# Pads of the self-attention's stacks filled in the prologue, and the first rows of maxima sent ahead of the third and fourth stack

## The chip, the cores and the metric

The kernel runs on one core of a Trainium2 chip. The metric is the device time of one execution in microseconds (us). Each kernel is executed several times and the median counts.

## What is computed

Two layers on x (2 batches, 1024 tokens, 256 features) and a context of 77 tokens per batch, everything in float32. The first layer is a cross-attention to the context, 16 heads of 16 features, with a residual. The second is a decoder block: self-attention over the 1024 tokens, cross-attention to the context, and a feed-forward part of 1024 features.

```python
# layer 0
x = merge(softmax(Q K^T / 4) V) + x                 # Q from x, K and V from the context
# layer 1
qn = layernorm(x);  x = x + out_proj(self_attention(qn))
xn = layernorm(x);  x = x + out_proj(cross_attention(xn, context))
xn = layernorm(x);  x = x + gelu(xn @ w1.T + b1) @ w2.T + b2
```

## The kernel before

**Attentions and steps.** The program is one stream for each engine, written out by hand and tied together by semaphores. It has three attentions: A0 (layer 0), A1 (self-attention) and A2 (cross-attention of layer 1). An attention works on groups of four heads (QUAD); there are eight groups, 0 to 3 for the first batch and 4 to 7 for the second. Each group has two query blocks of 512 tokens, so there are 16 query blocks q, with q = 2g and 2g + 1 in group g. In A0 a step t is one query block: four score matmuls (line 813) into ST, four exponentials on ScalarE (line 947), the product with the values (line 829) into PV one step later, and the transposed result (line 778) one step after that. A0 has steps 0 to 15. A1 has eight steps for each query block, 128 in all.

**Stacks.** The scores are made with a stacked operand: six bands of 16 rows, which are parts of the queries split into bfloat16 pieces, and three more rows that hold the negated row maxima. TensorE thus subtracts the maximum within the score matmul. The bands of a group ("stack g") are read back from DRAM (`q_parts`) by six DMAs of 128 KB each (line 596). A0 has four stack buffers: stacks 0 and 1 lie in the tile V, stacks 2 and 3 in the tile `stacks`. The query parts are made in the prologue by `proj_q0` for four token blocks tb of 512 tokens, two chunks each. Each chunk is split on ScalarE, VectorE and (for tb = 3, by `ring_split_by`) GpSimd, and stored to `q_parts` by one DMA of 384 KB (line 563). GpSimd's two operations for a chunk are at lines 1308 and 1314.

**Maxima and rows.** A side task ("max", u) makes scores of 128 queries against the 77 keys for the four heads of a group (line 761, four matmuls) into SM, and VectorE reduces them (line 1063). Four such units (u = 4q to 4q + 3) give the maxima of query block q. GpSimd splits them into three parts (lines 1281 to 1287, written to `mp`), TensorE transposes these (line 772), VectorE copies them to `mrow` (line 1073), and SyncE (SP) sends them into the stack by a DMA of 12 KB (line 634). This is the side task ("rows", q), called "row q" below. The scores of step q wait for it. A step t of A0 has the units u = 12 + 4t to 15 + 4t and row t + 2. Units 0 to 11 and rows 0 and 1 come before step 0, in the order u0 to u5, row 0, u6 to u9, row 1, u10, u11. The first unit of a group waits for the six DMAs of its stack: u8 for stack 1, u16 (the first of step 1) for stack 2, u24 (step 3) for stack 3, u32 (step 5) for stack 4.

**Order of SP's queue.** All of these DMAs are issued by SP, one after the other. The order in front of A0 is the list BEFORE_A0; the other engines walk the same list and take only what is theirs, so moving a ("stack", ...) entry moves nothing but DMAs of SP:

```python
BEFORE_A0 = [("proj_k0", 0), ("proj_q0", 0), ("keys", "a0"), ("proj_q0", 1), ("stack", "a0", 0), ("vals_c", 0),
             ("values", "a0", 0), ("stack", "a0", 1), ("proj_q0", 2), ("stack", "a0", 2), ("proj_q0", 3),
             ("side", A0, 0, len(A0.before)), ("stack", "a0", 3)]
```

For SP, ("proj_q0", tb) means that it waits until each of the two chunks is split and then stores it. Within a step t SP sends row t + 2, then does the step's chores (in steps 0 to 3 a load of 512 KB of x into X, line 540), then the stack that has come due (stack 4 in step 2, stack 5 in step 4, stack 6 in step 6, stack 7 in step 8).

**Pads.** The rows of a stack between and behind the bands have to hold constants. `pad` (line 1185) fills 32 partitions by 2048 floats on GpSimd; `padded` counts `pad_ready` up. The pads that A0 needs are filled at the very start. Those of A1 for the key buffers Kst[0] and Kst[1] and the query buffer Qst[0], which A0 does not use, are filled in A0's steps 0, 1 and 2 by the chores ("pads", "a1", n), two fills each; part 3 fills nothing. GpSimd does a step's maxima first and then its chores. The rest of A1's pads come after A0.

Of the kernel before, what the change touches and what calls it, by code (L numbers as in the profile page):

```python
# [38 lines left out]
NB = TOK // BLK  # L39
TPB = BLK // P  # L40
QUAD = 4
# [6 lines left out]
SROWS = len(BANDS) * HD  # L48
# [31 lines left out]
def one_in_two(first, work):  # L80
# [5 lines left out]


UNDER_A0 = {
    **{n: [("load", n), ("pads", "a1", n)] for n in range(NB)},
    8: [("load", 4), ("load", 5)],  # L90
    9: [("x1", 0)],
    10: [("norm", 0, 0), ("x1", 1), ("load", 6), ("load", 7)],
# [44 lines left out]
class Attention:  # L137
# [61 lines left out]
    def chores(self, t):  # L199
# [3 lines left out]
A0 = Attention(0, 1, CTX, lead=12, rows_ahead=2, rows_at=0, buffers=4, banks=4, under=UNDER_A0,  # L203
               split_by=("pool", "dve"), lag=(0, 1))
A1 = Attention(1, SEQ // P, P, lead=26, rows_ahead=1, rows_at=4, buffers=3, banks=2, under=UNDER_A1,
               split_by=("pool", "pool"), lag=(1, 2))
# [9 lines left out]


BEFORE_A0 = [("proj_k0", 0), ("proj_q0", 0), ("keys", "a0"), ("proj_q0", 1), ("stack", "a0", 0), ("vals_c", 0),
             ("values", "a0", 0), ("stack", "a0", 1), ("proj_q0", 2), ("stack", "a0", 2), ("proj_q0", 3),
             ("side", A0, 0, len(A0.before)), ("stack", "a0", 3)]  # L220
BEFORE_A1 = [("stack", "a1", 0), ("vals_s", 0), ("x1", 2), ("vals_s", 1), ("x1", 3),
             ("norm", 0, 2), ("side", A1, 0, 2), ("t_ln1", 2),
             ("norm", 0, 3), ("side", A1, 2, 4), ("t_ln1", 3), ("pads", "a1", NB)]
SPREAD = [(stage, tb, i, 1) for stage, tb in (("proj_q1", 2), ("proj_k1", 2), ("proj_q1", 3), ("proj_k1", 3))
          for i in range(KC)]
BEFORE_A1 += [w for i, chunk in enumerate(SPREAD) for w in (("side", A1, 2 * i + 4, 2 * i + 6), chunk)]
# [21 lines left out]
def xattn_kernel(nc, xT_d, x_d, cT_d, ident_d, cols_d, rows_d, wq0, wk0, wv0, sa_w, so_w,  # L248
# [8 lines left out]
    with ctx:  # L257
# [3 lines left out]
        def sem(name):  # L261
            return ctx.enter_context(nc.semaphore(name))
# [16 lines left out]
        Kst = [stacks[:, n, 0] for n in range(A1.buffers)]  # L279
        Qst = [stacks[:, n, 1] for n in range(A1.buffers)]  # L280
# [108 lines left out]
        st_done = sem("st_done")  # L389
# [776 lines left out]
        def _(pool):  # L1166
# [4 lines left out]
            def step(ins):  # L1171

                ins.then_inc(pool_step, 1)
                steps[0] += 1
                pool.wait_ge(pool_step, steps[0])

            def space():

                used[0] += 1
                return gp.memset(spacer[:, used[0]:used[0] + 1], 0.0)  # L1180


            def pad(tile, first, value):

                step(gp.memset(tile[first:first + 32].bitcast(FP32), value))  # L1185

            def padded():

                step(space())
                space().then_inc(pad_ready, 1)  # L1190
                step(space())
# [8 lines left out]
            step(gp.memset(prob[64:P, :, :, :], 0.0))  # L1200
            step(gp.memset(nexp[:, :], -0.5))
            padded()

            def stationary(att, g):


                if g >= 2:
                    pool.wait_ge(pv_done, att.t0 + (g - 1) * HALVES * att.kt)
                elif att is not A0:
                    old = ATT[BEFORE[att.name]]  # L1210
                    pool.wait_ge(pv_done, old.t0 + (NG - 1 + g) * HALVES * old.kt)
                    if att is A2:

                        step(space())
                        step(gp.memset(Vst[64:P, g % 2, 0, :, :], 0.0))
                        step(gp.memset(Vst[0:CTX, g % 2, 0, :, HD:HD + 1], 1.0))
                if att is A0 and g == 0:
                    pool.wait_ge(v_ready, PER["vals_c"])
                if att.whole:
                    if g % QUAD == 0:  # L1220
                        pool.wait_ge(*READ["vals_s", 2 * (g // QUAD) + 1, TPB - 1])
                    gp.tensor_copy(Vst[:, g % 2, :, :, 0:HD], V[:, g].rearrange("p k (h d) -> p k h d", h=QUAD)) \
                        .then_inc(vst_ready, 1)
                else:
                    b, h0 = g // QUAD, (g % QUAD) * QUAD
                    src = VC[att.name][0:CTX, b, h0 * HD:(h0 + QUAD) * HD]
                    gp.tensor_copy(Vst[0:CTX, g % 2, 0, :, 0:HD], src.rearrange("p (h d) -> p h d", h=QUAD)) \
                        .then_inc(vst_ready, 1)

            def pads(att, part):  # L1230

                step(space())
                if att is A1:
                    if part < 2:
                        pad(Kst[part], 32, 1.0)
                        pad(Kst[part], SROWS, 1.0)
                    elif part == 2:
                        pad(Qst[0], 32, 0.0)
                        pad(Qst[0], SROWS, 0.0)
                        padded()  # L1240
                    elif part == NB:
                        pool.wait_ge(st_done, A0.steps * QUAD)
                        pad(Qst[1], 32, 0.0)
                        pad(Qst[2], 32, 0.0)
                        pad(Kst[2], 32, 1.0)
                        pad(Kst[2], SROWS, 1.0)
                        padded()
                    step(space())
                    return
                pool.wait_ge(st_done, (att.t0 - (2 - part) * HALVES * A1.kt) * QUAD)  # L1250
                if part == 0:
                    pad(Kst[2], SROWS, TWO_ONES)
                    pad(Qst[2], SROWS, 0.0)
                elif part == 1:
                    pad(Qst[0], SROWS, 0.0)
                    pad(Kst[0], SROWS, 0.0)
                else:
                    pad(Qst[1], SROWS, 0.0)
                padded()
# [57 lines left out]
            def chore(w):  # L1317
                if w[0] == "pads":
                    pads(ATT[w[1]], w[2])
                elif w[0] == "values":  # L1320
                    stationary(ATT[w[1]], w[2])
                elif w[0] in ("x1", "stats"):
                    rsqrt(0 if w[0] == "x1" else w[1], w[-1])
# [81 lines left out]
```

## Time and profile before

| | |
|---|---|
| median of 3 runs | 814.62 us (814.15 to 816.78) |
| profiled execution, its own time | 815.85 us |
| span of its profile | 814.1 us |
| TensorE busy | 730.4 us (90%) |
| VectorE busy | 532.9 us (65%) |
| ScalarE busy | 441.7 us (54%) |
| GpSimd busy | 154.4 us (19%) |
| bytes moved by DMA | 59.54 MB |
| mean granted clock of TensorE | 0.952 |
| A0, steps 0 to 15, begins at | 47.2 us of the span |

The span is the time from the first to the last recorded instruction of one execution; what lies around it (815.85 less 814.1, 1.75 us) does not change with the program's order. A granted clock of 1.00 is 2.4 GHz, one of 0.50 is 1.2 GHz.

### The profile page before, as it was taken

What the parts mean: (1) busy time and instruction counts of PE and PEld (TensorE: products, weight loads), DVE (VectorE), ACT (ScalarE), POOL (GpSimd) and SP (SyncE); (2) the same over time, 40 slices, a digit from 0 to 9 for tenths busy, and PEclk for the clock granted to TensorE, in tenths of its full rate; (3) what the DMA queues carried; (4) which work ended last, traced back from release to release, by engine and by line L of the source; (5) the groups of instructions that cost most, each with busy time, mean ns of one, the idle gap of its engine ahead of it and who ended that gap; (6) DMA issues with size and microseconds to landing.
All of it is one profiled execution on the core that took longest, in us unless ns stands there. A gap on an engine that the chain in (4) does not pass through costs nothing.

```text
span 814.1 us, 13571 instructions
## 1 busy us (share of the span) xinstructions
PE 730.4 (90%) x5200; PEld 358.8 (44%) x5200; DVE 532.9 (65%) x851; ACT 441.7 (54%) x802; POOL 154.4 (19%) x341
## 2 busy tenths in 40 slices
PE   7568798388799999999999999997979997999998
PEld 3334444235233333333443433332444564556767
DVE  3546863697599999999889998870478775230001
ACT  4346453021488888888667766675645644323120
POOL 7344330341000000000001103141043223030000
PEclk9779899698899999999999999998999998999999
DMA  8967615535905040312205010016254700000001
GB/s 275 187 158 150 140 64 203 126 123 200 150 11 80 4 72 12 59 25 42 41 2 81 1 25 2 21 39 99 41 144 87 145 11 2 1 6 20 26 14 39
DMA packets 40751, 59.54 MB, mean 73 GB/s; under 512 B 8560, under 2 KB 23664, under 8 KB 40688
## 3 DMA queue, kind: packets, MB, share of 16 engines
q1 hardware_dynamic: 40400, 58.61, 32.1%
q8 instruction: 41, 0.67, 0.4%
q14 instruction: 22, 0.18, 0.1%
q10 hardware_dynamic: 288, 0.08, 0.0%
HBM read 36.31 MB, written 21.44 MB: 71 GB/s over the span
## 4 chain that ended last, share of the span: by engine, by line
PE 56%; DVE 20%; DMA 11%; SPq 4%; ACT 3%; issue 3%; POOL 2%; DVEq 0%; POOLq 0%; ACTq 0%
PE PV L829 14%; DVE nm L1060 13%; PE ST L813 11%; PE ST L721 5%; PE ST L717 5%; PE SM L756 5%; PE SM L708 3%; DMA stacks<-k_rows 3%; PE SM L698 2%; SPq L554 2%; DMA V<-mrow 2%; PE PV L721 2%; PE PV L717 2%; PE SM L702 2%; PE SM L778 2%
## 5 line engine op out<-in xcount | busy, mean ns | idle before, releaser
L947 ACT ACTIVATE prob<-ST 128x512 f32<-128x512 f32 (+1 forms) x640 | 349.7, 596 | 169.0 <-PE ST L813 160.1
L1060 DVE TENSOR_REDUCE nm<-SM 128x2 f32<-128x1024 f32 x256 | 308.8, 1221 | 24.1 <-PE SM L756 22.5
L829 PE MATMUL PV<-prob,Vst 128*32 128x256 f32 (+1 forms) x2304 | 205.0, 428 | 6.3 <-ACT prob L947 3.3
L813 PE MATMUL ST<-stacks 64*128 64x512 f32 (+1 forms) x608 | 172.0, 486 | 4.4 <-DMA stacks<-mrow 2.0
L756 PE MATMUL SM<-stacks 64*128 64x512 f32 x512 | 111.1, 429 | 25.6 <-DMA stacks<-k_rows 16.6
L813 PEld LDWEIGHTS ST<-stacks 64*128 64x128 f32 (+1 forms) x608 | 62.1, 174 | 140.0 <-ACT prob L947 102.6
L1063 DVE TENSOR_REDUCE nm<-SM 128x4 f32<-128x308 f32 x128 | 57.9, 471 | 48.5 <-PE SM L761 47.4
L829 PEld LDWEIGHTS PV<-prob,Vst 128*32 128x32 f32 x2304 | 46.3, 109 | 96.9 <-issue 70.4
L756 PEld LDWEIGHTS SM<-stacks 64*128 64x128 f32 x512 | 50.0, 190 | 47.9 <-issue 23.5
L1015 DVE TENSOR_TENSOR X<-ST,X 128x256 f32<-128x256 f32 x18 | 7.5, 422 | 90.5 <-PE ST L721 73.7
L936 ACT ACTIVATE pvT<-PV 128x512 f32<-128x512 f32 x48 | 28.7, 599 | 32.7 <-PE PV L829 32.6
L717 PE MATMUL ST<-fm,V 128*128 128x512 f32 x96 | 42.6, 593 | 0.3 <-ACT fm L918 0.3
L1275 POOL CAST mp<-na 128x16 fp32r<-128x16 f32 x16 | 3.2, 198 | 201.1 <-DVE na L1095 201.1
L1301 POOL TENSOR_TENSOR X<-X,bc 128x256 f32<-128x256 f32 x48 | 34.2, 742 | 30.2 <-DVE A L1045 30.2
L761 PE MATMUL SM<-stacks 96*128 96x77 bf16 x384 | 30.2, 205 | 6.7 <-DMA stacks<-q_parts 3.9
L761 PEld LDWEIGHTS SM<-stacks 96*128 96x128 bf16 x384 | 26.1, 104 | 22.2 <-issue 7.8
L778 PE MATMUL SM<-ident,pvT 128*128 128x128 f32 x192 | 32.0, 293 | 2.6 <-ACT pvT L936 1.0
L1185 POOL MEMSET stacks<- 32x2048 f32 x18 | 32.5, 1805 | 1.0
L698 PE MATMUL SM<-fm,early 128*128 128x512 f32 x64 | 31.0, 607 | 0.0
L778 PEld LDWEIGHTS SM<-ident,pvT 128*128 128x128 f32 x192 | 22.1, 148 | 12.7 <-issue 4.2
L717 PEld LDWEIGHTS ST<-fm,V 128*128 128x128 f32 x96 | 18.1, 190 | 21.7 <-issue 20.8
L698 PE MATMUL ST<-fm,early 128*128 128x512 f32 x48 | 24.9, 650 | 2.1 <-DVE Vc L1010 1.8
(114 smaller groups left out, 703.0 us busy)
## 6 DMA issues: line engine op xcount, KB each, us to landing
stacks<-q_parts SPq DMA_DIRECT2D x72, 128.0 KB, 4.8
q_parts<-split SPq DMA_DIRECT2D x16, 384.0 KB
q_rows<-parts SPq DMA_DIRECT2D x24, 256.0 KB
k_rows<-parts SPq DMA_DIRECT2D x24, 256.0 KB
stacks<-q_rows SPq DMA_DIRECT2D x16, 384.0 KB
stacks<-k_rows SPq DMA_DIRECT2D x16, 384.0 KB
V<-q_parts SPq DMA_DIRECT2D x24, 128.0 KB, 4.7
fm<-in_xT SPq DMA_DIRECT2D x4, 512.0 KB, 7.9
```

Source lines behind the costliest of these rows:

```text
L698: last = mm(ps[:, 0:width], weight[:, k, w0 + i * P:w0 + (i + 1) * P], src[:, k, c0:c0 + width], start=(k == 0), stop=(k == KC - 1))
L717: last = mm(ps[:, 0:BLK], w_1[:, k, i * P:(i + 1) * P], fm[:, k, tb * BLK:(tb + 1) * BLK], start=(k == 0), stop=(k == KC - 1))
L721: last = mm(ps[:, 0:DIM], hid[tb % 2][:, f, i * P:(i + 1) * P], w_2[:, f, :], start=(f == 0), stop=(f == FF // P - 1))
L756: last = mm(ps[:, s * BLK:(s + 1) * BLK], Q[rows, n, c0:c0 + P], Kst[g % att.buffers][rows, n, c * BLK:(c + 1) * BLK], start=True, stop=True)
L761: last = mm(ps[:, h * CTX:(h + 1) * CTX], Q[0:SROWS, h, c0:c0 + P], keys_of(att, g, h, 0)[0:SROWS], start=True, stop=True)
L778: last = nc.tensor.transpose(ps[:, n * P:(n + 1) * P], pvT[:, which % 2, n * P:(n + 1) * P], ident[:, :])
L813: mm(ST[0:att.keys, n % 3, :], keys_of(att, g, h, kt), QST[att.name][g % att.buffers][rows, at, j * BLK:(j + 1) * BLK], start=True, stop=T ...
L829: last = mm(PV[h * 32:(h + 1) * 32, queries], Vst[:, g % 2, kt, h, :], prob[:, t % 2, h, queries], start=(kt == 0 and first == 0), stop=(k ...
L947: act_fn(prob[0:att.keys, t % 2, h, :], ST[0:att.keys, n % 3, :], ACT.Exp, scale=SCALE if att.whole else 1.0).then_inc(exp_done, 1)
L1060: ins = vec.tensor_reduce(nm2[:, q % 2, c, tile, 2 * n:2 * n + 2], ps.rearrange("p (s k) -> p s k", s=2), AX.X, ALU.max, negate=True)
L1063: ins = vec.tensor_reduce(nm[:, q % 2, v, :], ps[:, 0:QUAD * CTX].rearrange("p (h k) -> p h k", h=QUAD), AX.X, ALU.max, negate=True)
L1301: ins = gp.tensor_tensor(X[:, t, :], X[:, t, :], bc[:, (B_SO, B_CO, B_F2)[n], :], ALU.add)
```

## The change

The chores ("pads", "a1", 0 to 3) leave A0's steps. Their six fills are done in the prologue instead, behind the kernel's own prologue fills, and `pad_ready` still reaches 3 after them. The chore behind A0 that fills the remaining pads keeps its place, and two tiny fills of a spacer around the fills fall away. In BEFORE_A0 stack 1 moves behind the stores of proj_q0's third and fourth block, and stack 2 moves behind the twelve units of maxima and the two rows, so that both rows are sent ahead of stacks 2 and 3.

```diff
 UNDER_A0 = {
-    **{n: [("load", n), ("pads", "a1", n)] for n in range(NB)},
+    **{n: [("load", n)] for n in range(NB)},
...
 BEFORE_A0 = [("proj_k0", 0), ("proj_q0", 0), ("keys", "a0"), ("proj_q0", 1), ("stack", "a0", 0), ("vals_c", 0),
-             ("values", "a0", 0), ("stack", "a0", 1), ("proj_q0", 2), ("stack", "a0", 2), ("proj_q0", 3),
-             ("side", A0, 0, len(A0.before)), ("stack", "a0", 3)]
+             ("values", "a0", 0), ("proj_q0", 2), ("proj_q0", 3), ("stack", "a0", 1),
+             ("side", A0, 0, len(A0.before)), ("stack", "a0", 2), ("stack", "a0", 3)]
 BEFORE_A1 = [("stack", "a1", 0), ("vals_s", 0), ("x1", 2), ("vals_s", 1), ("x1", 3),
              ("norm", 0, 2), ("side", A1, 0, 2), ("t_ln1", 2),
-             ("norm", 0, 3), ("side", A1, 2, 4), ("t_ln1", 3), ("pads", "a1", NB)]
+             ("norm", 0, 3), ("side", A1, 2, 4), ("t_ln1", 3), ("pads", "a1", 0)]
...
             step(gp.memset(nexp[:, :], -0.5))
             padded()
+            for tile, value in ((Kst[0], 1.0), (Qst[0], 0.0), (Kst[1], 1.0)):
+                pad(tile, 32, value)
+                pad(tile, SROWS, value)
+            padded()
...
                 step(space())
                 if att is A1:
-                    if part < 2:
-                        pad(Kst[part], 32, 1.0)
-                        pad(Kst[part], SROWS, 1.0)
-                    elif part == 2:
-                        pad(Qst[0], 32, 0.0)
-                        pad(Qst[0], SROWS, 0.0)
-                        padded()
-                    elif part == NB:
-                        pool.wait_ge(st_done, A0.steps * QUAD)
-                        pad(Qst[1], 32, 0.0)
-                        pad(Qst[2], 32, 0.0)
-                        pad(Kst[2], 32, 1.0)
-                        pad(Kst[2], SROWS, 1.0)
-                        padded()
-                    step(space())
+                    pool.wait_ge(st_done, A0.steps * QUAD)
+                    pad(Qst[1], 32, 0.0)
+                    pad(Qst[2], 32, 0.0)
+                    pad(Kst[2], 32, 1.0)
+                    pad(Kst[2], SROWS, 1.0)
+                    padded()
                     return
```

## Rows read from the trace of the kernel before

**Rows 1.** Busy time by stretch: A1's body; busy us (instructions) per engine.

```profile
220.00:520.00 300.00, 292.87 (x2629) 115.33 (x2627) 278.63 (x300) 231.89 (x432) 23.39 (x52) 0.99 0.21 34
```

**Rows 2.** Chain that ended last: start us, us, what; ahead of A0's step 0.

```profile
27.36 5.46 DMA V<-q_parts
...
37.44 9.63 DMA V<-mrow
```

**Rows 3.** Timeline of SP's DMA issues: start us, us, issues (SPq).

```profile
25.12 5.47 SPq L596 DMA_DIRECT2D V<-q_parts  x12
...
31.76 3.16 SPq L596 DMA_DIRECT2D stacks<-q_parts  x6
34.97 1.08 SPq L563 DMA_DIRECT2D q_parts<-split  x2
...
59.80 0.42 SPq L540 DMA_DIRECT2D X<-in_x  x1
60.41 3.39 SPq L596 DMA_DIRECT2D V<-q_parts  x6
...
77.70 0.70 SPq L634 DMA_DIRECT2D V<-mrow  x1
```

**Rows 4.** Timeline of TensorE: start us, us, instructions, [idle before, releaser].

```profile
38.45 0.68 PE L761 MATMUL SM<-stacks,V 96*128 96x77 bf16 x8 [0.92 <-DMA V<-q_parts]
...
39.97 0.70 PE L761 MATMUL SM<-stacks,V 96*128 96x77 bf16 x8
47.20 0.62 PE L813 MATMUL ST<-V,stacks 128*77 128x512 bf16 x1 [6.53 <-DMA V<-mrow]
...
51.03 0.47 PE L761 MATMUL SM<-stacks 96*128 96x77 bf16 x4
...
54.44 0.38 PE L813 MATMUL ST<-V,stacks 128*77 128x512 bf16 x1
...
62.88 0.38 PE L772 MATMUL SM<-identb,mp 128*12 128x128 bf16 x4 [1.71 <-POOL mp L1287]
...
69.44 0.54 PE L813 MATMUL ST<-stacks 128*77 128x512 bf16 x1
...
77.94 0.38 PE L813 MATMUL ST<-stacks 128*77 128x512 bf16 x1
...
81.41 0.38 PE L813 MATMUL ST<-V,stacks 128*77 128x512 bf16 x1
```

**Rows 5.** Timeline of GpSimd (POOL), same columns.

```profile
12.83 3.51 POOL L1200 MEMSET prob<- 64x4096 f32 x1
...
16.57 0.29 POOL L1180 MEMSET spacer<- 128x1 f32 x3
...
29.81 2.39 POOL L1308 TENSOR_TENSOR parts<-parts,split 128x512 f32<-128x512 f32 x2 [6.47 <-ACT split L880]
32.16 2.26 POOL L1314 TENSOR_TENSOR split<-parts,split 128x512 bf16<-128x512 f32 x2
...
57.60 3.66 POOL L1185 MEMSET stacks<- 32x2048 f32 x2
```

**Rows 6.** Timeline of VectorE (DVE), the prologue, same columns.

```profile
13.04 0.69 DVE L1102 TENSOR_TENSOR parts<-parts,split 128x512 f32<-128x512 f32 x1 [2.65 <-ACT split L880]
...
19.56 0.69 DVE L1102 TENSOR_TENSOR parts<-parts,split 128x512 f32<-128x512 f32 x1 [0.55 <-ACT split L880]
```

**Rows 7.** Busy time by stretch; the last three columns: granted clock, DMA share, GB/s.

```profile
32.50:37.50 5.00, 3.00 (x36) 2.42 (x36) 2.96 (x8) 0.37 (x1) 2.77 (x6) 0.50 1.08 137
...
40.00:43.70 3.70, 0.67 (x9) 0.49 (x8) 1.24 (x3) 0.00 (x0) 1.02 (x5) 0.50 1.06 187
```

**Rows 8.** Busy time by stretch within A0, same columns as rows 7.

```profile
60.00:62.00 2.00, 1.17 (x13) 0.30 (x5) 1.22 (x3) 1.44 (x3) 1.78 (x5) 1.00 0.31 62
...
66.00:68.00 2.00, 0.41 (x5) 0.17 (x3) 0.48 (x1) 1.07 (x2) 1.54 (x9) 1.00 1.09 183
...
71.00:72.00 1.00, 1.00 (x8) 0.05 (x4) 0.44 (x1) 0.29 (x1) 0.00 (x0) 0.50 0.73 188
```

## Prediction

> **What bounds the kernel now.** I read the busy time by stretch first. In A1's body TensorE is busy 292.87 of 300 us and VectorE 278.63 [rows 1]. Nothing in the change touches that stretch. The change can only move the moment at which A1 begins, and I found no piece of the chain between A0 and A1 that hangs on an absolute time. So I treat a shift within A0 as a shift of the end.
>
> Then the chain of waits up to A0. It goes from the landing of stack 0 at 27.36 + 5.46 = 32.82 us through eight maxima to the DMA of row 0, issued at 37.44 and landed 9.63 us later, at 47.07 [rows 2]. SP's issues say why 12 KB take that long: stack 2 (31.76) and the last two stores of `q_parts` (34.97) went into the same queue just ahead of it [rows 3]. TensorE's timeline shows the end of that wait, 6.53 us of idle time before step 0 at 47.20 [rows 4].
>
> Last the steps. Step 7 begins at 77.94 and step 8 at 81.41, an undisturbed step of 3.47 us. Step 2 begins at 54.44, step 5 at 69.44 and step 7 at 77.94: 15.00 and 8.50 us for three and two steps, where 10.41 and 6.94 would do [rows 4]. In the first stretch TensorE waits for GpSimd's split of the maxima (1.71 us ahead of 62.88, one of three such waits [rows 4]), because two fills of 3.66 us together stand before it [rows 5]. The second stretch has no wait of that kind, but the clock there is 0.50 [rows 8]. So both edits aim at waits that the trace shows: at most 23.50 less 5 x 3.47, 6.15 us, from the pads and the slow clock behind them, and some of the 6.53 us from the rows.
>
> **The change, part by part.**
>
> *Fills in the prologue.* GpSimd's prologue ends at 16.57 + 0.29 = 16.86 us, and its next work that anyone waits for is the split of the last query chunks at 29.81 [rows 5]. Six fills at 3.66 us for two are 11.0 us, and the spacers of a `padded` 0.3 [rows 5]. That ends at about 28.2; the small copy of the values behind it is not needed before PV of step 0. So this costs nothing, with 1.6 us of cover. If the cover is gone, the stores of `q_parts` are late by the excess, and stack 1 behind them. VectorE splits query chunks at the same time. Its 0.69 us operation takes 0.69 us at 13.04, under GpSimd's fill of 3.51 us at 12.83, and 0.69 us at 19.56, beside no GpSimd work [rows 5, 6]. By the trace the two do not slow each other. The Trainium skill, GPSIMD Engine Reference, section 1 (the table's row on SBUF interfaces), speaks against this: GpSimd shares its SBUF interfaces with VectorE and contends with VectorE instructions that have two SBUF inputs, as these subtractions have. It gives no price, and the trace does not agree with it for this pair; I keep zero.
>
> *Stack 1 behind the stores.* Before, its last landing releases unit 8 at 38.45 [rows 4]. After, SP first waits for GpSimd's second chunk, ready at 32.16 + 2.26 = 34.42 [rows 5], issues its store in 0.54 (1.08 for two [rows 3]), and begins stack 1 at 34.96. Stack 0, issued into a nearly empty queue, shows the price: first issue at 25.12 [rows 3], landing at 32.82 [rows 2], 7.7 us. That gives 42.66; call it S = 42.6, against 38.45. The bounds come from the pace: six DMAs of 128 KB are 786 kB, 5.7 us at 137 GB/s and 4.2 at 187 [rows 7] (stack 1 before: 38.45 less 32.82, 5.6 us). With the fast pace S is 41.2; with the store's bytes wholly in front of the slow one it is 43.5.
>
> *Rows 0 and 1, and step 0.* TensorE takes its work in order. Row 0 is ready at 37.4 as before, but is issued behind stack 1 and lands with it, at S + 0.2. That no longer decides, because step 0 now waits for units 8 to 11. Units 8 and 9 start at 38.45 and units 10 and 11 end at 39.97 + 0.70 = 40.67 [rows 4], 2.2 us: step 0 begins at S + 2.2 = 44.8, 2.4 us earlier than 47.20. Row 1 is issued about 2.1 us behind S and must be there for step 1, 3.4 us after step 0's start, so it has 3.5 us. Row 8, issued at 77.70, was there for step 8 at 81.41, 3.7 us later with no wait of its own [rows 3, 4]. I take no cost, at most 0.2.
>
> *Stacks 2 and 3 behind row 1.* This is where the gain is lost. SP is blocked until row 1 is copied and sent, so stack 2's first issue is at S + 2.8 = 45.4, where it was at 31.76 [rows 3]. By stack 0's 7.7 us it lands at 53.1. Step 1's first maximum reads it 3.8 us behind step 0's start (51.03 less 47.20 [rows 4]), at 48.6: TensorE waits 4.5 us there, where it waited for nothing before. From that maximum to step 2 took 3.41 us (54.44 less 51.03 [rows 4]); if TensorE is at the slow clock throughout, I estimate 1.3 more (steps 5 and 6, with one slow stretch, took 1.56 us too much). Step 2 would begin at 56.5 to 57.8. But row 2 is later: SP issues stack 3's six DMAs before it, and its 12 KB lie in the queue behind stack 3, which follows stack 2 by 3.7 to 5.6 us. I take 5.0, between the pair of stacks that ran back to back (5.6) and the one that ran behind stores, because these two run back to back but with SP's issues in between. Row 2 lands at 53.1 + 5.0 + 0.2 = 58.3. Step 2 begins at 58.3 instead of 54.44, 3.9 us late.
>
> *No fills in steps 0 to 2.* Step 3 and 4 then follow at 3.47 us each, as their rows have room. Step 5 does not: it needs row 5 and, for unit 32, stack 4. In an undisturbed step the row goes out 3.23 us behind the start (77.70 less 74.47, which is 77.94 less 3.47 [rows 3, 4]) and the load of X 0.75 later, 4.0 behind step 2's start. Before, this load went out at 59.80, stack 4 at 60.41, and row 5 behind them was in time for 69.44, at most 9.6 us after the load [rows 3, 4]. So step 5 begins at 4.0 + 9.4 = 13.4 us behind step 2, not at 10.4; the pads' 4.6 us shrink to 15.0 less 13.4, 1.6. Steps 5 and 6 keep their 8.50 if the clock falls again and save 1.56 if it does not. Before, an idle stretch like that of 66 to 68 us was followed by 0.50 at 71 to 72, while one in 60 to 62 was not [rows 8]. TensorE will now stand for 3.0 us in one piece before step 5, more than in either, so I take nothing here. From step 7 on the order and the waits are those of before.
>
> The sum: 3.9 late at step 2, less 1.6, is 2.3 us late. On the profiled execution this is a span of 814.1 + 2.3 = 816.4 and a time of 818.1; that execution lay 1.2 us above the median, so on the median 814.62 + 2.3 = 816.9 us.
>
> **The bounds.** The pace of a stack enters four times: in S, in stack 2, in stack 3 and in the wait before step 5. With 4.2 us everywhere, and the clock kept at step 5, S is 41.2, row 2 lands at 41.2 + 2.8 + 6.2 + 4.2 + 0.2 = 54.6 (0.2 late), step 5 follows by about 12.5 (2.5 gained) and 1.56 is saved: 3.9 us faster. With 5.6 everywhere, S = 43.5, and step 2 at the slow clock (1.5 more), it is 5.4 us slower.
>
> **The rivals.** A measurement of this kernel can tell 0.3%, 2.4 us, from no change.
>
> *A, the forecast:* stacks late, pads' time returned to the queue; 0 to 4 us slower, 816.9 likeliest. Chance 0.55, of which about 0.33 lies under 2.4 us and 0.22 above.
>
> *B, faster:* the queue hands over a stack at 3.8 us or less. Then row 2 and stack 4 come 1.2 us earlier each time, and the four terms give back 4.8 us: 2.5 us faster, 812.1; at an even 3.3 us it is 810. For it: the 187 GB/s of the stack that ran from 40.0 to 43.7 [rows 7]. Against it: stacks 0 and 1 at 137 GB/s [rows 7] and 7.7 us for a lone stack [rows 2, 3]. It decides below 3.8 us for a stack. Chance 0.15.
>
> *C, slower still:* TensorE's clock. It now stands idle three times, for 5 us before S, 4.5 us in step 1 and 3.0 us before step 5. If each is followed by a stretch at 0.50 that reaches into the next undisturbed step, steps 2 and 6 cost 1.5 us more each: 4 to 5.4 us slower, 819.5. For it: the 0.50 at 71 to 72, behind an idle stretch [rows 8]. Against it: the slow stretch there was over within the step. The Trainium skill, TensorE: Matmul & The Clock Gate, section on oscillation, says that a wait for a DMA lets the throttle return and the next matmuls start cold; the trace agrees in the row just named. Chance 0.20 (with 0.02 for fills that outrun their cover in the prologue).
>
> *D, no change:* the clock stays at full speed behind step 5 and the lateness of stack 3 is the smaller one; the two edits cancel within 1.5 us. 814 to 815. Chance 0.10.
>
> Faster: B, 0.15. Within 0.3%: 0.33 of A and D, 0.43. Slower: 0.22 of A and C, 0.42. The range that leaves out 2 in 10 is 812.4 to 819.8 us; A's own is 814.6 to 818.6.
>
> **What would show it.** Step 0 at 44.8 (earlier than 47.2), waiting for unit 8 and not for row 0. A wait for a DMA of `stacks` of 4 to 5 us at the first maximum of step 1. Step 2 near 58.3, behind row 2. No wait for GpSimd at the transposed maxima in steps 2 to 4, and instead a wait for a row or for stack 4 before step 5. GpSimd's fills over by 28.5 and its split of the last chunk still at 29.8. The prediction is wrong if stacks pass the queue much faster when SP has issued less ahead of them, if step 1's maximum does not wait, or if step 5 follows step 2 by 10.4 us.

## The result, and the profile after

The changed kernel takes 823.44 us (median of 12 runs, 820.61 to 827.39) against 815.6 us for the kernel before (12 runs beside them, 813.52 to 819.97): a ratio of 1.008, 95% interval 1.006 to 1.0101, 7.8 us slower. The forecast was 2.3 us slower, with a range up to 819.8. The sign is right; the size is outside the range.

The page of the profile after first. This execution took 827.39 us, the longest of the twelve, so its span is read for places and not for the total.

```profile
span 825.6 us, 13560 instructions
PE 733.6 (89%) x5200; PEld 360.2 (44%) x5200; DVE 532.8 (65%) x851; ACT 441.8 (54%) x802; POOL 153.8 (19%) x332
PE 55%; DVE 19%; DMA 11%; SPq 7%; ACT 4%; issue 3%; POOL 1%; DVEq 0%; ACTq 0%; POOLq 0%
```

TensorE is busy 3.2 us longer than before with the same 5200 matmuls (733.6 against 730.4 us); the other engines are busy as long as before within 0.6 us. What answers to rows 4, TensorE's timeline around A0's first steps (start us, us, instructions, [idle before, releaser]):

```profile
42.80 0.68 PE L761 MATMUL SM<-stacks,V 96*128 96x77 bf16 x8 [4.09 <-DMA V<-q_parts]
...
44.43 0.63 PE L813 MATMUL ST<-V,stacks 128*77 128x512 bf16 x1
...
53.33 0.42 PE L761 MATMUL SM<-stacks 96*128 96x77 bf16 x4 [4.86 <-DMA stacks<-q_parts]
...
58.89 0.41 PE L813 MATMUL ST<-V,stacks 128*77 128x512 bf16 x1 [0.39 <-DMA V<-mrow]
...
62.39 0.38 PE L813 MATMUL ST<-V,stacks 128*77 128x512 bf16 x1
...
73.78 0.65 PE L813 MATMUL ST<-stacks 128*77 128x512 bf16 x1 [4.30 <-DMA stacks<-mrow]
```

The lines show four things. Unit 8 waits for stack 1 until 42.80, and step 0 begins at 44.43, earlier than before. The first maximum of step 1 waits 4.86 us for stack 2, where nothing waited before. Step 2 begins at 58.89 behind row 2. And the three waits for GpSimd are gone, but step 5 waits 4.30 us for row 5 and begins at 73.78. SP's issues (rows 3) explain each:

```profile
29.33 6.14 SPq L563 DMA_DIRECT2D q_parts<-split  x4
35.51 3.15 SPq L596 DMA_DIRECT2D V<-q_parts  x6
38.76 6.48 SPq L634 DMA_DIRECT2D V<-mrow  x2
45.41 5.96 SPq L596 DMA_DIRECT2D stacks<-q_parts  x12
51.47 0.72 SPq L634 DMA_DIRECT2D V<-mrow  x1
...
63.37 0.42 SPq L540 DMA_DIRECT2D X<-in_x  x1
63.98 2.81 SPq L596 DMA_DIRECT2D V<-q_parts  x6
66.84 0.72 SPq L634 DMA_DIRECT2D stacks<-mrow  x1
```

Stack 1 now goes out at 35.51 behind all four stores, stacks 2 and 3 in one piece from 45.41, and row 2 behind them at 51.47. Row 5 (66.84) is issued behind the load of x (63.37) and stack 4 (63.98). The chain of waits (start us, us, what) shows how long the two 12 KB rows then lie behind a stack, as row 0 did before [rows 2]:

```profile
51.47 7.38 DMA V<-mrow
...
66.84 6.90 DMA stacks<-mrow
```

GpSimd's timeline (rows 5) shows that the six fills cost nothing where they now stand. They end at 27.90, and the split of the last chunks begins at 30.47, released by ScalarE as before:

```profile
16.82 11.08 POOL L1185 MEMSET stacks<- 32x2048 f32 x6
27.96 0.29 POOL L1180 MEMSET spacer<- 128x1 f32 x3
...
30.47 2.39 POOL L1303 TENSOR_TENSOR parts<-parts,split 128x512 f32<-128x512 f32 x2 [1.89 <-ACT split L880]
```

VectorE's two-input operation took 0.69 us under these fills too, as in rows 6:

```profile
20.21 0.69 DVE L1102 TENSOR_TENSOR parts<-parts,split 128x512 f32<-128x512 f32 x1 [0.54 <-ACT split L880]
```

### The profile page after: what moved, and what is told of

The parts are those of the page before. It is cut to its first block, busy times and chain, and to the rows that moved or that the text cites. A ratio compares the mean times of both kernels' runs of the same rounds, so it can differ in the third digit from the quotient of the medians.

```text
span 825.6 us, 13560 instructions
## 1 busy us (share of the span) xinstructions
PE 733.6 (89%) x5200; PEld 360.2 (44%) x5200; DVE 532.8 (65%) x851; ACT 441.8 (54%) x802; POOL 153.8 (19%) x332
## 4 chain that ended last, share of the span: by engine, by line
PE 55%; DVE 19%; DMA 11%; SPq 7%; ACT 4%; issue 3%; POOL 1%; DVEq 0%; ACTq 0%; POOLq 0%
PE PV L829 14%; DVE nm L1060 13%; PE ST L813 11%; PE ST L721 5%; PE ST L717 5%; PE SM L756 4%; SPq L554 4%; PE SM L708 3%; DMA stacks<-k_rows 3%; DMA V<-mrow 2%; PE SM L698 2%; DMA stacks<-mrow 2%; PE PV L721 2%; PE PV L717 2%; PE SM L761 2%
## 5 line engine op out<-in xcount | busy, mean ns | idle before, releaser
L717 PE MATMUL ST<-fm,V 128*128 128x512 f32 x96 | 42.6, 593 | 0.3 <-ACT fm L918 0.3
L1276 POOL CAST mp<-nm 128x16 bf16<-128x16 f32 x32 | 6.3, 198 | 117.3 <-DVE nm L1063 117.3
```

Of the source, the lines that this page charges most:

```text
L717: last = mm(ps[:, 0:BLK], w_1[:, k, i * P:(i + 1) * P], fm[:, k, tb * BLK:(tb + 1) * BLK], start=(k == 0), stop=(k == KC - 1))
```

## The experiments

Each kernel is compared with the kernel before on the same chip. "Step 2" is the moment at which step 2's first score matmul starts in that kernel's profile. The pads are those of the changed kernel unless the edit says otherwise.

**The fills alone.** BEFORE_A0 as before.

```diff
-             ("values", "a0", 0), ("proj_q0", 2), ("proj_q0", 3), ("stack", "a0", 1),
-             ("side", A0, 0, len(A0.before)), ("stack", "a0", 2), ("stack", "a0", 3)]
+             ("values", "a0", 0), ("stack", "a0", 1), ("proj_q0", 2), ("stack", "a0", 2), ("proj_q0", 3),
+             ("side", A0, 0, len(A0.before)), ("stack", "a0", 3)]
```

> The fills in the prologue, SP's order as before. Queue theory: the fills cost nothing in the prologue (split of the last chunks still begins near 30 us), the waits for GpSimd in steps 2 to 4 vanish, but step 5 is held by row 5 behind stack 4: step 5 begins 13.4 to 14.9 us behind step 2 instead of 15.0. Time 0 to 2.5 us below before, 1.5 likeliest. Rival, the fills were the whole of the stall: step 5 follows step 2 by 10.4 us and the time falls by about 6 us. Rival, the moved fills are what made the changed kernel slow (they hold up VectorE or the late stores): 3 us or more above before.

817.49 us against 817.69, ratio 1.0004 (0.9972 to 1.0036): no change. TensorE's timeline has two waits left between steps 1 and 6, both at step 5. The first line is the start of step 2:

```profile
53.72 0.38 PE L813 MATMUL ST<-V,stacks 128*77 128x512 bf16 x1
...
68.34 0.41 PE L813 MATMUL ST<-stacks 128*77 128x512 bf16 x1 [4.07 <-DMA stacks<-mrow]
...
68.92 0.42 PE L761 MATMUL SM<-stacks,V 96*128 96x77 bf16 x4 [0.17 <-DMA V<-q_parts]
```

SP's issues show what lay ahead of row 5:

```profile
58.17 0.42 SPq L540 DMA_DIRECT2D X<-in_x  x1
58.77 2.70 SPq L596 DMA_DIRECT2D V<-q_parts  x6
61.52 0.72 SPq L634 DMA_DIRECT2D stacks<-mrow  x1
```

Step 2 began at 53.72, so step 5 followed by 14.6 us; in the kernel before it is 15.0 in the first profile and 15.6 in the mean of five (table below). Nearly all of the stall that the fills had caused came back as a wait for row 5. Both rivals fall: the fills were not worth 6 us, and moving them did not cost 3 us or more (the interval reaches from 2.3 us faster to 2.9 us slower).

**The order alone.** The kernel before with the changed BEFORE_A0; the fills stay in steps 0 to 2.

```diff
-             ("values", "a0", 0), ("stack", "a0", 1), ("proj_q0", 2), ("stack", "a0", 2), ("proj_q0", 3),
-             ("side", A0, 0, len(A0.before)), ("stack", "a0", 3)]
+             ("values", "a0", 0), ("proj_q0", 2), ("proj_q0", 3), ("stack", "a0", 1),
+             ("side", A0, 0, len(A0.before)), ("stack", "a0", 2), ("stack", "a0", 3)]
```

> SP's order of the changed kernel, the fills left in steps 0 to 2. Queue theory: step 1's first maximum waits about 4.9 us for stack 2 as in the changed kernel, step 2 begins near 58.5; the fills of steps 0 and 1 hide under that wait and those of step 2 under the hold before step 5. So within 1.5 us of the changed kernel, 7 to 9 us above before. Rival, the two edits add: 13 us above before, since the fills' stall comes on top. Rival, the order is harmless and the fills did it: within 1 us of before.

824.05 us against 817.69, ratio 1.0058 (1.003 to 1.0085), 6.4 us slower by the medians, a little under the 7 to 9 us expected. Its interval is 2.5 to 7.0 us. The order alone makes the loss, and the two edits do not add.

```profile
54.51 0.42 PE L761 MATMUL SM<-stacks 96*128 96x77 bf16 x4 [4.78 <-DMA stacks<-q_parts]
59.97 0.65 PE L813 MATMUL ST<-V,stacks 128*77 128x512 bf16 x1 [0.28 <-DMA V<-mrow]
72.25 0.38 PE L772 MATMUL SM<-identb,mp 128*12 128x128 bf16 x4 [1.36 <-POOL mp L1287]
76.51 0.65 PE L813 MATMUL ST<-stacks 128*77 128x512 bf16 x1 [2.92 <-DMA stacks<-mrow]
```

One wait for GpSimd is still there, 1.36 us, and the wait for row 5 is 2.92 us, by about as much less than the 4.30 us of the changed kernel: the one hides in the other.

**Stack 2 alone moved.** Stack 1 back in its old place.

```diff
-             ("values", "a0", 0), ("proj_q0", 2), ("proj_q0", 3), ("stack", "a0", 1),
+             ("values", "a0", 0), ("stack", "a0", 1), ("proj_q0", 2), ("proj_q0", 3),
```

> As the changed kernel, but stack 1 back in its old place; stack 2 stays behind the two rows. Queue theory: stack 1 lands near 38.5, row 0 behind the stores near 43.4, step 0 then; row 1 is sent near 40.6, stack 2 lands near 48.9, so step 1's first maximum waits only 1.5 to 2 us; row 2 behind stack 3 lands near 54.2, step 2 begins there, as before. Time within 1.5 us of before, 6 us below the changed kernel. Rival, the move of stack 2 alone does the harm wherever stack 1 stands: step 1 waits 4 to 5 us and the time is 6 us or more above before.

817.12 us against 817.69, ratio 0.9995 (0.9962 to 1.0028). The time is as expected, the place is not:

```profile
42.95 0.62 PE L813 MATMUL ST<-V,stacks 128*77 128x512 bf16 x1 [1.40 <-DMA V<-mrow]
...
51.37 0.42 PE L761 MATMUL SM<-stacks 96*128 96x77 bf16 x4 [4.52 <-DMA stacks<-q_parts]
```

Step 0 began 4.3 us earlier than in the first profile of before, but stack 2 landed at 51.3 and not at 48.9, and step 1 waited 4.5 us instead of 1.5 to 2. Step 2 began at 56.34, 1.1 us behind the mean of before. What row 0 gained, stack 2 took back.

**Stack 1 alone moved.** Stack 2 directly behind it, ahead of the maxima and rows.

```diff
-             ("values", "a0", 0), ("proj_q0", 2), ("proj_q0", 3), ("stack", "a0", 1),
-             ("side", A0, 0, len(A0.before)), ("stack", "a0", 2), ("stack", "a0", 3)]
+             ("values", "a0", 0), ("proj_q0", 2), ("proj_q0", 3), ("stack", "a0", 1), ("stack", "a0", 2),
+             ("side", A0, 0, len(A0.before)), ("stack", "a0", 3)]
```

> As the changed kernel, but stack 2 directly behind stack 1, ahead of the maxima and rows; only stack 1's move behind the stores is left. Queue theory: stack 1 lands near 42.8, row 0 behind stack 2 near 47.7, step 0 0.5 us later than before, no wait at step 1's first maximum, step 2 near 55. Time within 1.5 us of before. Rival, a late stack 1 does the harm: 4 us or more above before.

821.11 us against 817.69, ratio 1.0035 (1.0006 to 1.0065). By the medians this is 3.4 us slower, more than the 1.5 us expected and less than the rival's 4; the interval, 0.5 to 5.3 us, excludes neither. Stack 1 was late by 5.8 us, not 4.4, and row 0 behind stack 2 later than planned:

```profile
44.28 0.68 PE L761 MATMUL SM<-stacks,V 96*128 96x77 bf16 x8 [7.00 <-DMA V<-q_parts]
...
50.65 0.62 PE L813 MATMUL ST<-V,stacks 128*77 128x512 bf16 x1 [4.53 <-DMA V<-mrow]
...
58.24 0.38 PE L813 MATMUL ST<-V,stacks 128*77 128x512 bf16 x1
```

Step 2 began at 58.24 and not near 55: 3.0 us behind the mean of before, where the changed kernel is 4.4 us behind. The way is another one. Row 0 lay behind stack 2 and held steps 0 and 1, and step 1's first maximum then waited for nothing. So stack 2's move alone costs nothing that these runs show, and stack 1's move alone carries a part of the loss. How large a part is not shown: against the 6.4 us of both moves on the same chip the intervals overlap.

**Two loads of x out of the way of stack 4.** The fills in the prologue, BEFORE_A0 as before.

```diff
-    **{n: [("load", n)] for n in range(NB)},
+    0: [("load", 0)], 1: [("load", 1)], 5: [("load", 2)], 7: [("load", 3)],
```

> The fills in the prologue, SP's order in the prologue as before, and the loads of x of steps 2 and 3 moved to steps 5 and 7, out of the queue around stack 4. In the kernel with the fills alone step 5 waited 4.07 us for row 5, 14.6 us behind step 2. Queue theory: one load of 512 KB ahead of stack 4 falls away, 1.5 us at the pace of the stores, so the wait shrinks to about 2.6 us and step 5 follows step 2 by 13.1 us; the time falls by about 1.5 us against the fills alone, 1 to 3 us below before. Rival, row 5 is late for a reason of its own (its own latency, a late split of the maxima): the wait stays near 4 us and the time that of before.

814.06 us against 817.07, ratio 0.9962 (0.9939 to 0.9984).

```profile
69.05 0.41 PE L813 MATMUL ST<-stacks 128*77 128x512 bf16 x1 [2.70 <-DMA stacks<-mrow]
```

The wait for row 5 fell from 4.07 to 2.70 us, and step 5 followed step 2 by 69.05 less 55.79, 13.3 us. In the nine profiles of kernels that have the fills in the prologue and a load of x just ahead of stack 4 that wait is 3.3 to 4.3 us. Row 5 is held by what lies ahead of it in the queue. By the medians the kernel is 3.0 us faster than before; the wait accounts for about 1.4 us of that, and where the rest comes from is not shown.

**Rows ahead of other work.** SP gets a list of its own; the other engines keep BEFORE_A0.

```diff
+SP_BEFORE_A0 = [("proj_k0", 0), ("proj_q0", 0), ("keys", "a0"), ("proj_q0", 1), ("stack", "a0", 0),
+                ("stack", "a0", 1), ("proj_q0", 2), ("side", A0, 0, 7), ("stack", "a0", 2),
+                ("side", A0, 7, len(A0.before)), ("proj_q0", 3)]
...
-    **{n: [("load", n)] for n in range(NB)},
+    0: [("stack", "a0", 3)], 4: [("load", 0)], 5: [("load", 1)], 6: [("load", 2)], 7: [("load", 3)],
```

> The fills in the prologue, and an order of SP's own that follows the queue theory: stack 1, the stores of the third block, row 0, stack 2, row 1, the stores of the fourth block, step 0's row 2, stack 3, and the loads of x in steps 4 to 7. Queue theory: row 0 lands near 40.5 and step 0 begins near 41 instead of 47.2; step 1 waits for row 1 behind stack 2, near 46; step 2 near 50 instead of 54.4; stack 4 has no load of x ahead of it, so step 5 near 62 to 64 instead of 69.4; time 5 to 8 us below before. Rival, the order of SP's queue is not what sets A0's early steps, or what is gained there is lost at the stores in front of A1: within 2 us of before.

814.32 us against 817.07, ratio 0.9955 (0.9928 to 0.9982), 2.8 us faster by the medians, less than expected. Step 0 began at 40.50, step 2 at 50.39 and step 5 at 63.26, all as planned, and 6.7, 4.1 and 6.2 us ahead of the first profile of before. Then the loads in steps 6 and 7 met stack 6, and step 9 waited 3.45 us (line 816 here is line 813, moved down by the new list):

```profile
45.59 0.41 PE L816 MATMUL ST<-V,stacks 128*77 128x512 bf16 x1 [2.03 <-DMA V<-mrow]
...
63.26 0.65 PE L816 MATMUL ST<-stacks 128*77 128x512 bf16 x1 [2.31 <-DMA stacks<-mrow]
...
82.29 0.41 PE L816 MATMUL ST<-V,stacks 128*77 128x512 bf16 x1 [3.45 <-DMA V<-mrow]
```

The version above, which only moves the fills and two loads, took 814.06 us on the same chip. What the new order gained in A0's first steps does not show in the time.

**The loads placed anew.**

```diff
-    0: [("stack", "a0", 3)], 4: [("load", 0)], 5: [("load", 1)], 6: [("load", 2)], 7: [("load", 3)],
+    0: [("stack", "a0", 3)], 3: [("load", 0), ("load", 1)], 5: [("load", 2)], 7: [("load", 3)],
```

> As the kernel with the rows ahead of other work, but the loads of x in steps 3 (two), 5 and 7 instead of 4 to 7. There, step 9 waited 3.45 us for row 9 behind stack 6 and two loads, and 4 us of the gain at step 7 were gone at A1's start. Queue theory: the wait at step 9 falls to 1.1 to 1.7 us as in the kernels with at most one load near stack 6, and the time falls to 4 to 6 us below before. Rival, what is gained in A0 is lost again in front of A1 whatever the order: step 9 improves, the time stays 2 to 3 us below before.

812.82 us against 817.3, ratio 0.995 (0.9919 to 0.9981), 4.5 us faster by the medians and the lowest ratio here, though its interval overlaps that of the version above and, at 1.6 to 6.6 us faster, does not exclude the rival's 2 to 3. The wait at step 9 fell to 1.11 us, as expected, but 1.11 us of waiting for row 7 arose at step 7:

```profile
74.52 0.41 PE L816 MATMUL ST<-stacks 128*77 128x512 bf16 x1 [1.11 <-DMA stacks<-mrow]
82.76 0.41 PE L816 MATMUL ST<-V,stacks 128*77 128x512 bf16 x1 [1.11 <-DMA V<-mrow]
```

**The two kernels again.** The changed kernel was timed a second time. There are six profiles of it and five of the kernel before.

> The changed kernel again, for a second profile and a second comparison. Queue theory: the places in A0 repeat (step 0 near 44.5, 4.9 us of wait at step 1's first maximum, step 2 near 58.5, step 5 held 4 us) and the time is 6 to 8 us above before. Rival, half of the first profile's 11.5 us arose behind A0 as scatter and does not repeat: the shift at the end is that at A1's first maxima, 5 to 7 us, give or take 2.

> The kernel before again, one look, for the scatter of a profile. The places in A0 repeat within 1 us. If the stretch of A1 near 630 us, where three of four other profiles lost 2 to 4 us against the first profile of before, is scatter of that first profile, it loses as much here; if it is owed to the edits, this profile agrees with the first one there.

> A third profile of the changed kernel, for the scatter. Its places in A0 have been steady (step 5 3.6 to 4.3 us later than in the first profile of before), its end has not (2.1 and 11.5 us later). If the loss behind A0 is systematic (the stores and stack loads in front of A1, steps at the slow clock), it shows again, 2 us or more between step 7 and the end; if scatter, less than 1 us or of the other sign.

> A fourth profile of the changed kernel, same reading as the third.

> A third profile of the kernel before, same reading: its steps in A0 within 1 us of the first two, its end 0 to 3 us later than in the first.

> A fifth profile of the changed kernel. If the 2 us that the changed kernel lost on average between A1's start and the end are owed to the edits, they show again; if they are scatter (a wait for a row at A2's start, long enough or not to let the clock fall), the loss from 614 us to the end is spread as in the profiles of before.

> A sixth profile of the changed kernel, with the same reading as the fifth: the loss from 614 us to the end repeats if the edits cause it, and is spread as in before if not.

> A fourth profile of the kernel before, same reading: scatter if it too loses 1 to 3 us against the first one between 614 us and the end.

> A fifth profile of the kernel before, with the same reading as the fourth: scatter if it too loses 1 to 3 us against the first one between 614 us and the end.

The second timing gave 824.22 us against 817.07, ratio 1.0086 (1.0057 to 1.0115). The profiles, in the order in which they were taken (step 2, step 5: start of the first score matmul; A1: start of A1's first maximum; all us):

| | step 0 | step 2 | step 5 | A1 | span |
|---|---|---|---|---|---|
| before, 1 | 47.20 | 54.44 | 69.44 | 157.02 | 814.1 |
| before, 2 | 48.00 | 55.24 | 70.53 | 158.79 | 815.7 |
| before, 3 | 47.39 | 53.72 | 69.47 | 157.21 | 816.2 |
| before, 4 | 48.13 | 55.18 | 71.50 | 159.51 | 819.7 |
| before, 5 | 50.60 | 57.59 | 73.38 | 160.86 | 818.0 |
| **mean** | 48.26 | 55.23 | 70.86 | 158.68 | 816.7 |
| changed, 1 | 44.43 | 58.89 | 73.78 | 164.36 | 825.6 |
| changed, 2 | 45.12 | 59.13 | 73.01 | 159.87 | 816.1 |
| changed, 3 | 45.15 | 59.67 | 74.33 | 161.19 | 820.8 |
| changed, 4 | 45.55 | 60.64 | 76.12 | 163.99 | 823.4 |
| changed, 5 | 44.77 | 59.66 | 73.80 | 164.29 | 820.5 |
| changed, 6 | 45.20 | 59.76 | 76.05 | 163.56 | 822.2 |
| **mean** | 45.04 | 59.63 | 74.52 | 162.88 | 821.4 |
| difference | -3.2 | +4.4 | +3.7 | +4.2 | +4.7 |

The loss is there at step 2 and is carried to the end. What the first profile of the changed kernel lost beyond that, behind A1's start, is scatter: from there to the end of the span it is 656.9 to 660.2 us in the five of before and 656.2 to 661.2 in the six of the changed kernel, 658.1 and 658.6 in the mean. The first profile of before, on which the prediction rests, has the shortest span of the five.

In two of the six (changed 4 and 6) step 2 ran at 1.2 GHz and took 5.1 us; in the other four it took 3.5. The busy time by stretch, with the granted clock in the third column from the end, of changed 1:

```profile
57.00:59.00 2.00, 1.61 (x13) 0.87 (x11) 1.35 (x3) 1.11 (x2) 0.00 (x0) 0.59 1.08 197
61.00:63.00 2.00, 2.00 (x25) 1.47 (x24) 1.36 (x4) 1.68 (x4) 0.15 (x2) 1.00 0.73 247
```

of changed 4:

```profile
59.00:61.00 2.00, 0.36 (x5) 0.24 (x6) 0.45 (x1) 0.42 (x1) 0.83 (x4) 1.00 1.11 222
61.00:63.00 2.00, 2.00 (x18) 0.66 (x15) 0.96 (x2) 1.14 (x2) 0.00 (x0) 0.50 0.86 283
```

and of changed 6:

```profile
59.00:61.00 2.00, 1.45 (x12) 0.72 (x10) 0.71 (x2) 1.08 (x2) 0.83 (x4) 0.50 0.84 214
61.00:63.00 2.00, 2.00 (x13) 0.37 (x11) 0.73 (x2) 0.69 (x2) 0.00 (x0) 0.50 0.71 243
```

In changed 6 the clock had not yet risen when step 2 began. In changed 4 it was at 1.00 ahead of step 2 and fell again within it. The waits that stood before, on TensorE's timeline of changed 4:

```profile
54.67 0.42 PE L761 MATMUL SM<-stacks 96*128 96x77 bf16 x4 [5.92 <-DMA stacks<-q_parts]
60.64 0.41 PE L813 MATMUL ST<-V,stacks 128*77 128x512 bf16 x1 [1.71 <-DMA V<-mrow]
```

The length of these waits does not tell the two kinds apart: in changed 6 they were 4.80 and 0.55 us, in changed 3, whose step 2 ran at 2.4 GHz, 5.69 and 1.15 us.

## Why the prediction was wrong in size

*The fills in the prologue:* right. They ended at 27.90 (28.2 forecast) and held up nobody; the kernel with the fills alone shows it.

*Stack 1 and step 0:* right. Unit 8 was released at 42.80 against S = 42.6, and step 0 began at 44.43 against 44.8 (mean of six 45.04).

*Stacks 2 and 3, step 2:* the mechanism was right and the size nearly so. Step 1's first maximum ran at 53.33 (53.1 forecast), step 2 began at 58.89 (58.3). Over all profiles the delay at step 2 is 4.4 us where the sum had 3.9.

*The fills' return:* this is the step that failed, "the pads' 4.6 us shrink to 15.0 less 13.4, 1.6". I had seen that row 5 would lie behind stack 4. But both parts of the 13.4 us were too small. The load of x goes out 4.0 us behind step 2's start in the sum, a figure read from a later step; it went out 4.45 behind it in the kernel with the fills alone (53.72 to 58.17) and 5.0 in the mean of the six profiles of the changed kernel (4.5 where step 2 ran at 2.4 GHz, 6.1 where it ran at 1.2). From that load to step 5 the sum has 9.4 us, read from an execution in which row 5 was in time by an unknown margin; it took 10.2 in the kernel with the fills alone (58.17 to 68.34) and 9.9 in the mean of six. So step 5 followed step 2 by 14.89 us in the mean of six, against 15.63 in the five of before: 0.7 returned instead of 1.6.

*The clock:* a part of that miss is rival C's, whose cost stood in the sum at nothing. It had a chance of 0.20, and in two of six executions step 2 ran at 1.2 GHz, at 1.6 us each. Without these two, step 5 would follow step 2 by 14.39 us, and 1.2 us would have returned.

These terms make 4.4 less 0.7, 3.7 us at step 5, where I had 2.3, and nothing is given back later: 4.2 at A1, 4.7 in the spans. Rival B had no support: stack 2 was not in before 7.9 us from its first issue (45.41 to 53.33), and the wait for it was 4.8 to 5.9 us in all profiles with the changed order. Rival D is excluded by the interval. C came nearest: its 4 to 5.4 us hold the 4.7 of the profiles, but not the 7.8 of the timed medians.

*The rest is open.* The medians of the timed runs say 7.8 us (interval 6.0 to 10.1 thousandths, 4.9 to 8.2 us) and, on another chip, 7.2. The profiles say 4.7, but single spans scatter over 814.1 to 819.7 and 816.1 to 825.6, so the mean difference is itself uncertain by about 3 us (twice the standard error, from these eleven spans). The two agree within that. The gap does not lie in a place behind A1's start that the profiles show. By the medians it lies on the side of before: the six profiled executions of the changed kernel took 823.3 us in the mean, like its timed runs (823.44 and 824.22), but the five of before 818.6, where the medians of its timed runs are 815.6 to 817.7.

The mean granted clocks on record point to TensorE's clock. It is 0.9487 over the 12 timed executions of the changed kernel and 0.9482 over the 8 later ones, and 0.9535 over the 25 of before beside those 8; in the profiled executions it is 0.9503 and 0.9516. Among the executions of either kernel those with the lower clock are the longer ones: a straight line through them gives 0.4 to 0.6 us for each 0.001. By that the 0.005 in the timed runs stand for 2 to 3 us, and the 0.0013 in the profiles for less than 1. This is an estimate from a correlation and no proof: a longer wait at 1.2 GHz also lowers the mean.

My range was too narrow because it came from the bounds of single terms and left out that executions of this kernel differ by several us. It was also added to the median of only three runs of before, 814.62, where 12 and more gave 815.6 to 817.7.

## What to carry to other kernels

When every transfer goes through one queue, moving a small urgent transfer ahead of a large one makes the large one late by all that the small one waits for: ask who reads the large one and when. Here step 0 began 3 us earlier, stack 2 was issued 13.7 us later (45.41 against 31.76), and it was needed one step behind row 0. Work that nobody needs yet is what should give way: with loads of x moved out from ahead of stack 4 the kernel was faster than before, by 3.0 us in its simplest form. A stall that is taken off one engine is worth only the distance to the next late thing, and that distance is not read from a profile in which the first stall hid it; a run that removes the first stall alone measures it.

## What the runs showed of the hardware

A row of 12 KB took 7.4 us from issue to landing behind stack 3, six DMAs of 128 KB, and the end of stack 2, and 9.6 us behind a stack and two stores [rows 2]: on this queue small transfers gained little on the large ones issued ahead of them. In the kernel with the fills alone row 5, issued at 61.52, was in when step 5 began at 68.34; the last DMA of stack 4, issued before it, landed at 61.05 + 7.74, 68.79 (chain of waits):

```profile
61.05 7.74 DMA V<-q_parts
```

A stack moved at 137 to 187 GB/s [rows 7], stores of the same bytes at about 350 GB/s, so the same 768 KB held the queue 2.2 us as a store and 4.2 to 5.7 us as a stack. The cause of the difference was not tried. The stretches of these, busy time and GB/s in the kernel before:

```profile
37.50:40.00 2.50, 1.27 (x14) 0.90 (x14) 1.54 (x4) 0.00 (x0) 0.84 (x4) 0.50 1.09 349
...
43.70:46.20 2.50, 0.00 (x0) 0.00 (x0) 0.00 (x0) 0.00 (x0) 0.00 (x0) 0.50 1.10 346
```

The Trainium skill, DMA: Bandwidth & Descriptors, section on queues, rings and completion order, says that each DMA engine consumes the descriptors of a ring in order, though completions may pass one another. The first half agrees with the waits for rows here, 7.4 and 9.6 us; the second agrees with row 5, which was in at least 0.4 us before a DMA issued ahead of it.
